# Attention and feed-forward layer on one core: queries in three buffers of two mirrored blocks, output projection as three rounded passes, three shared PSUM banks

## The reference, cut to what matters

```
xn = _layernorm(x, axis=-1)
q = einsum('bld,dhk->blhk', xn, Wq)            # 16 heads of 64
latent = einsum('bld,dc->blc', xn, Wkv_down)   # 64
k = einsum('blc,chk->blhk', latent, Wk_up)
v = einsum('blc,chk->blhk', latent, Wv_up)
attn = softmax(where(causal, einsum('bqhd,bkhd->bhqk', q, k) / sqrt(64), min))
y = einsum('bhqk,bkhd->bqhd', attn, v)
x = x + einsum('bqhd,hdo->bqo', y, Wout) + tanh(xn @ weight @ aux1 @ aux2 + bias)
```

## Time and profile before

| | |
|---|---|
| runs | 2118.16, 2114.27, 2122.21 us, median 2118.16 |
| the profiled execution | 2116.38 us, of which the recorded span is 2114.6 us |
| granted TensorE clock, mean | 0.997 |
| busy share of the span | PE 97%, DVE 71%, POOL 62%, ACT 49% |

### The profile page before, as it was taken

How to read it: one execution, slowest core, us unless ns; L and a number is a source line. 1 busy time by engine, 2 the same in 40 slices (tenths; PEclk the granted TensorE clock), 3 DMA queues, 4 the chain that set the end, 5 groups by cost and what they waited for, 6 DMA issues and landing times.

```text
span 2114.6 us, 32583 instructions
## 1 busy us (share of the span) xinstructions
PE 2042.4 (97%) x9912; PEld 1265.4 (60%) x9912; DVE 1501.8 (71%) x3743; ACT 1044.1 (49%) x1947; POOL 1319.9 (62%) x1163
## 2 busy tenths in 40 slices
PE   6999999999999999999999999999999999999997
PEld 5655666656666566656565656665666556666654
DVE  5868766787677776777676776778757687677662
ACT  4544554545545454544554545455554445545443
POOL 0666666666667565665666666667666566666765
PEclk9999999999999999999999999999999999999999
DMA  3111111211112111111111111111111111111111
GB/s 109 26 36 51 31 45 43 55 37 38 43 36 59 42 36 41 40 48 44 34 49 39 52 34 39 46 42 51 29 49 47 36 50 31 44 52 36 32 31 41
DMA packets 66999, 91.18 MB, mean 43 GB/s; under 512 B 12304, under 2 KB 33680, under 8 KB 66832
## 3 DMA queue, kind: packets, MB, share of 16 engines
q1 hardware_dynamic: 66832, 89.11, 15.3%
HBM read 45.55 MB, written 8.91 MB: 26 GB/s over the span
## 4 chain that ended last, share of the span: by engine, by line
PE 72%; DVE 16%; issue 4%; DMA 2%; ACT 2%; SPq 1%; POOL 0%; POOLq 0%; DVEq 0%
PE ps L860 20%; PE ps L874 12%; PE ps L843 10%; PE ps L911 10%; PE ps L846 9%; PE ps L814 8%; DVE maxima L1093 3%; PE ps L901 3%; DVE ps L1088 2%; DVE norm L1110 2%; DVE xn L1172 2%; DVE rows L1104 1%; DVE q_lo L1196 1%; DMA rows<-norm 1%; ACT q_hi L1064 1%
## 5 line engine op out<-in xcount | busy, mean ns | idle before, releaser
L1225 POOL TENSOR_TENSOR p_sum<-p_sum,probs 128x512 f32<-128x512 f32 x672 | 867.6, 1316 | 326.3 <-ACT probs L1010 325.5
L1010 ACT ACTIVATE probs<-ps 128x512 f32<-128x512 f32 x1152 | 673.2, 597 | 494.3 <-PE ps L846 467.1
L1088 DVE CUSTOM_DVE_ANT_0 ps<-ps,causal 128x256 f32<-128x256 f32 (+3 forms) x1024 | 495.5, 502 | 215.3 <-PE ps L874 206.5
L860 PE MATMUL ps<-probs,latent 128*64 128x512 f32 x2304 | 541.1, 601 | 0.0
L843 PE MATMUL ps<-q_hi,k_hilo 128*128 128x512 f32 x1152 | 499.4, 434 | 9.3 <-ACT probs L1010 9.1
L874 PE MATMUL ps<-k_hilo,q_hi 128*128 128x512 f32 (+3 forms) x1536 | 481.4, 368 | 19.1 <-DVE maxima L1088 11.0
L1093 DVE TENSOR_REDUCE maxima<-ps 128x1 f32<-128x512 f32 x512 | 351.4, 686 | 158.9 <-PE ps L874 156.7
L846 PE MATMUL ps<-q_lo,k_ones 65*128 65x512 f32 x1152 | 456.0, 396 | 0.0
L874 PEld LDWEIGHTS ps<-k_hilo,q_hi 128*128 128x128 f32 x1536 | 277.6, 189 | 176.2 <-issue 55.4
L1225 POOL TENSOR_TENSOR p_sum<-probs 128x512 f32<-128x512 f32 x224 | 292.2, 1321 | 131.5 <-ACT probs L1010 130.6
L1213 POOL TENSOR_SCALAR_AFFINE_SELECT probs<-probs 128x512 f32<-128x512 f32 x256 | 162.9, 639 | 316.3 <-ACT probs L1010 314.8
(11 more groups left out here) (93 smaller groups left out, 1488.5 us busy)
## 6 DMA issues: line engine op xcount, KB each, us to landing
q_hi<-q_hi SPq DMA_DIRECT2D x256, 128.0 KB, 2.3
norm<-recips SPq DMA_DIRECT2D x256, 128.0 KB, 2.9
x_in<-in_L_attn_x_bld SPq DMA_DIRECT2D x8, 1024.0 KB, 5.5
out_x<-acc SPq DMA_DIRECT2D x64, 128.0 KB, 1.7
q_lo<-rows SPq DMA_DIRECT2D x128, 4.0 KB
rows<-norm SPq DMA_DIRECT2D x128, 4.0 KB
recips<-rows SPq DMA_DIRECT2D x128, 4.0 KB
probs<-in_L_attn_Wq SPq DMA_DIRECT2D x1, 1024.0 KB, 8.0
```

The source lines that it names most:

```text
L860: last = nc.tensor.matmul(y_bank[g * LATENT:(g + 1) * LATENT, :], latent[par][:, key_block(unit, s), :], probs[:, t % PT_SLOTS, g * BANK:( ...
L1010: nc.scalar.activation(probs[:, t % PT_SLOTS, g * BANK:(g + 1) * BANK], st_bank[(2 * t + g) % ST_BANKS], ACT.Exp).then_inc(exp_done, 1)
L1088: nc.vector.tensor_tensor_reduce(bank, bank, causal[:, BANK - w:BANK], 1.0, LOWEST, ALU.add, ALU.max, maxima[:, unit % 4, h, 0:1]).then_in ...
L1225: nc.gpsimd.tensor_tensor(sums, other, probs[:, slot, part], ALU.add).then_inc(pool_done, 1)
```

## The change

1. **Order of units.** `HALF_BLOCKS` = (3,4), (2,5), (1,6), (0,7). Two units of mirrored blocks are a half (9 steps always), and a pair of blocks is done for the first octet, then for the second. Queries are made a half at a time (2 blocks, 8 heads) into one of three buffers, two halves ahead. A Q item now makes 4 heads of 2 blocks: 12 matmuls of 256 columns instead of 6 of 512. There are as many Q items (128), copies, remainders and DMAs as before, with the same elements.
2. **Output projection.** O is done in three rounded passes with `wvo_hi`, `wvo_lo`, `split_hi`, `split_lo`: 12 rounded matmuls of 256 columns for a unit instead of 4 in plain float32. For it NM writes back into `y`, then ACT rounds `y` to `split_hi` (HI), then DVE subtracts (LO) into `split_lo`; each once for a unit, 128x512. The prologue makes `wvo_lo` with four DVE subtractions.
3. **Banks.** Values (Y), preparation (P0) and small products (P1) share banks 5, 6 and 7; the planner gives each product the bank that is free first (`HOMES`, `takes`, `leaves`), and PE waits for the last reader of that bank alone (`bank_left`). A batch of PV steps may run across the end of a unit, since the next unit takes another bank.
4. **Planner.** `BATCH` 5, `LEAD` 13, other assumed times, an O after NM, HI and LO; the load of the next batch is put at step 30 of a batch instead of 32.

```diff
-SEGMENT_BLOCKS = [[3, 7, 4, 0], [5, 6, 2, 1]]
+HALF_BLOCKS = [(3, 4), (2, 5), (1, 6), (0, 7)]
...
-ST_BANKS, PT_SLOTS, Y_SLOTS, SUM_SLOTS = 2, 7, 3, 2
+PT_SLOTS, Y_SLOTS, SPLIT_SLOTS, SUM_SLOTS, Q_BUFS = 7, 3, 2, 2, 3
+HOMES = {"ST": (0, 1), "MAX": (2, 3, 4), "Y": (5, 6, 7), "P0": (5, 6, 7), "P1": (5, 6, 7)}
...
-BATCH = 4
+BATCH = 5
 SOON = 60
-LEAD = 12
+LEAD = 13
...
             elif kind == "NM":
+                self.multiplied[key] = self.run("DVE", when, DVE_TIME[kind])
+                if key < SPLIT_SLOTS or key - SPLIT_SLOTS in self.out:
+                    self.after(self.multiplied[key], "HI", key)
+            elif kind == "HI":
+                self.after(self.run("ACT", when, ACT_TIME[kind]), "LO", key)
+            elif kind == "LO":
                 self.normal[key] = self.run("DVE", when, DVE_TIME[kind])
                 self.outs.append((self.n_st / 2, key))
...
-            if s == block_of(u):
+            if s == block_of(u) and len(HOMES["Y"]) == 1:
                 return n, True
...
-            def p1_ready():
-                if n_p1:
-                    pe.wait_ge(p1_free, n_p1)
+            def bank_left(bank):
+
+                kind, key = last_use.get(bank, (None, None))
...
+                elif kind == "Y":
+                    pe.wait_ge(y_copied, key + 1)
+                elif kind in ("T", "K", "Q"):
+                    pe.wait_ge(p0_free, count.residual(kind, key) + 1)
...
                 elif kind in ("O0", "O"):
 
                     if kind == "O0":
-                        p1_ready()
-                        pe.wait_ge(y_normal, key + 1)
-                    for j in (0, 1) if kind == "O0" else (2, 3):
-                        last = nc.tensor.matmul(p1_bank[:, 0:D], norm[:, key % Y_SLOTS, j * P:(j + 1) * P],
-                                                wvo[:, octet_of(key) * PAIRS + j, :],
-                                                start=(j == 0), stop=(j == PAIRS - 1))
+                        p1_bank = take_bank("O", key)
+                        pe.wait_ge(norm_lo, key + 1)
+                    p1_bank = ps[:, bank_of["O", key], :]
+                    slot, first = key % SPLIT_SLOTS, octet_of(key) * PAIRS
+                    last = three_passes(
+                        p1_bank[:, 0:D],
+                        lambda a, j: (split_hi, split_lo)[a][:, slot, j * P:(j + 1) * P],
+                        lambda b, j: (wvo_hi, wvo_lo)[b][:, first + j, :],
+                        chunks=(0, 1) if kind == "O0" else (2, 3), of=PAIRS)
...
                     t, unit, s = key
                     act.wait_ge(pv_done, t + 1)
                     if unit >= Y_SLOTS:
-                        act.wait_ge(y_normal, unit - Y_SLOTS + 1)
+                        act.wait_ge(norm_lo, unit - Y_SLOTS + 1)
...
+                elif kind == "HI":
+                    act.wait_ge(y_normal, key + 1)
+                    if key >= SPLIT_SLOTS:
+                        act.wait_ge(p1_full, count.p1("O", key - SPLIT_SLOTS) + 1)
+                    nc.scalar.activation(split_hi[:, key % SPLIT_SLOTS, :], y[:, key % Y_SLOTS, :],
+                                         ACT.Copy).then_inc(norm_hi, 1)
...
+                elif kind == "LO":
+                    slot = key % SPLIT_SLOTS
+                    dve.wait_ge(norm_hi, key + 1)
+                    nc.vector.tensor_tensor(split_lo[:, slot, :], y[:, key % Y_SLOTS, :],
+                                            split_hi[:, slot, :].bitcast(F32),
+                                            ALU.subtract).then_inc(norm_lo, 1)
...
-        run(first_plan(), [ps[:, 6, :], ps[:, 0, :], ps[:, 1, :]], load_all, make_constants)
-        run(body_plan(B), [ps[:, 6, :]])
+        run(*first_plan(), load_all, make_constants)
+        run(*body_plan(B))
```

More of the change, by code:

```diff
@@ L274, in place_max @@
         self.plan.append(("MAX", self.maxima[self.n_max]))
+        self.takes("MAX", "MAX", self.maxima[self.n_max])
         slot = max(0.42 * w + 16, 112)
@@ L301, in place_p1_half @@
         self.plan.append(("O", u))
-        self.out.add(u)
-        self.p1_free = self.run("DVE", self.on_pe("O", ready), DVE_TIME["O"])
+        done = self.on_pe("O", ready)
+        self.out[u] = done
+        if u + SPLIT_SLOTS in self.multiplied:
+            self.after(max(done, self.multiplied[u + SPLIT_SLOTS]), "HI", u + SPLIT_SLOTS)
+        self.leaves("O", u, self.run("DVE", done, DVE_TIME["O"]))
     def place_f(self, ready):
@@ L308, in place_f @@
         self.n_f += 1
-        self.p1_free = self.run("DVE", self.on_pe("F", ready), DVE_TIME["F"])
-        self.after(self.p1_free, "FT", key)
+        self.takes("P1", "F", key)
+        end = self.run("DVE", self.on_pe("F", ready), DVE_TIME["F"])
+        self.leaves("F", key, end)
+        self.after(end, "FT", key)
     def place_r(self, ready):
@@ L315, in place_r @@
         self.plan.append(("R", u))
-        self.p1_free = self.run("ACT", self.on_pe("R", ready), ACT_TIME["R"])
-        self.after(self.p1_free, "RG", u)
+        self.takes("P1", "R", u)
+        end = self.run("ACT", self.on_pe("R", ready), ACT_TIME["R"])
+        self.leaves("R", u, end)
+        self.after(end, "RG", u)
     def place_p0(self, ready):
@@ L414, in build @@
             st = [c for c in usable if c[1] is None]
-            idle_act = self.free["ACT"] < now + 300
+            idle_act = self.free["ACT"] < now + 100
             late = max(due, key=lambda c: step - c[1], default=None)
@@ L439, in body_plan @@
 def body_plan(batches):
-    return Order(batches).build()
+    order = Order(batches)
+    plan = order.build()
+    return plan, order.bank
 def first_plan():
@@ L1273, in sync_program @@
                                  ).then_inc(x_loaded, 16)
-            for j in range(PAIRS):
-                sp.wait_ge(q_twice[j], 32 * sum(k == "Q" and key[1] == j for k, key in plan))
+            for i in range(Q_BUFS):
+                for j in range(2):
+                    uses = sum(k == "Q" and key[0] % Q_BUFS == i and key[1] == j for k, key in plan)
+                    if uses:
+                        sp.wait_ge(q_twice[i][j], 32 * uses)
             turned = sum(k == "MT" for k, _ in plan)
@@ L1280, in sync_program, with run @@
             if outputs:
-                for s in range(2):
-                    sp.wait_ge(stored[s], 16 * outputs // 2)
-        def run(plan, p0_banks, load=None, make_constants=None):
+                for s in range(BLOCKS // 2):
+                    sp.wait_ge(stored[s], 16 * outputs // (BLOCKS // 2))
+        def run(plan, bank_of, load=None, make_constants=None):
             with nc.Block() as block:
```

449 lines of the change are left out of this document (260 added, 189 removed).

## The result

The changed kernel takes 2100.57 us (median of 5, 2095.43 to 2103.03); the kernel before, in the same rounds, 2120.61 (median of 5). The ratio is 0.990, with a 95% interval from 0.988 to 0.992: 20 us less, where 54 were forecast. The direction was right and the time lies within the range for 8 in 10 (2040 to 2110), but outside the forecast's own (2046 to 2086): most of the forecast gain is missing. The profiled execution took 2102.5 us, with a span of 2100.8.

The account below looks back on a forecast made before the run. PE, busy for 97% of the span, was taken to set the pace. 2116.38 - 64 (PE work) + 20 (LO) - 15 (banks) + 5 (end) = 2062.4, median 2064 us; own range 2046 to 2086, 8 in 10 2040 to 2110.

Parts of the forecast that it names:

- What bounds the kernel: Whole body: PE, busy 97% of the span, sets the pace; cuts count fully unless what replaces them makes PE wait.
- Part 1: Output projection on PE: twelve rounded matmuls at 0.118 us replace eight recorded ones at 0.216; 40 us saved.
- the rival of the weight loads: O and Q on PE: weight loads of 189 ns in a row set the pace; 2281 us, chance 0.02.
- Their busy share: Weight loads on PE: 1280 more loads of 189 ns take their busy share from 60% to 73%.
- Parts 2 and 3: PE: twelve query matmuls instead of six, 3 us more; fewer changes of the array's form, 27 us saved.
- Part 4: HI on ACT hidden; LO adds 130 us on DVE, PE's waits for maxima grow by a half: +20 us.
- the second rival: NM, HI, LO queues: the planned order slips, 0.38 us lost on PE a unit; 2108 us, chance 0.10.
- LO as PE's limit: DVE's queue: LO ahead of maxima costs PE its 1.02 us each; 2190 us, chance 0.11.
- Part 5: Shared banks: PE's waits of Q and O for a bank, 28 us, go by half; -15 us.
- Part 6: Kernel's end: POOL's last steps +1.4 us, HI and LO behind NM +1.2, PE's 2.4 saved hidden; +5 us.
- for longer than 1.03: Sign for the end: R of the last unit waits longer for POOL than 1.03 us.

Follow-up runs that it names:

- e2: Changed kernel with the output projection as before (8 float32 matmuls, no HI, no LO), order built anew; 2093.9 us, ratio to before 0.987.
- e9: Changed kernel, same order, LO replaced in place by two bn_stats of one SBUF input, lower halves left out of O; 2061.4 us, ratio to before 0.972.
- e1: Changed kernel, same order, without DVE's LO; O reads the upper halves in both roles; 2051.2 us, ratio to before 0.967.
- e8: Kernel before with the layer-norm chain of batches 1 to 7 left out; 2116.5 us, ratio to before 0.9995.
- e3: Changed kernel, same order, layer-norm chain after bn_aggr left out in batches 1 to 7; 2069.1 us, ratio to before 0.976.
- e11: Changed kernel with float32 output projection as before and the layer norm's Newton steps on POOL; 2073.8 us, ratio to before 0.978.
- e4: Changed kernel with one bank each for values, preparation and small products; 2122.9 us, ratio to before 1.002.
- e12: Changed kernel, same order, without both LO and the layer-norm chain of batches 1 to 7; 2030.6 us, ratio to before 0.959.
- e14: e11 with Newton links spread behind POOL's additions and the first batch's chain on DVE; 2078.6 us, ratio to before 0.982.
- e7: Changed kernel with LO on POOL instead of DVE, order built anew; 2085.2 us, ratio to before 0.985.

## Why the prediction was wrong in size, step by step

- **What bounds the kernel** held: PE paces the body. What was not held is the other half of that sentence, "unless what replaces it makes PE wait".
- **Part 1**, 40 us less work: 39 (e2 against after, by counts and pitches). The rounded matmuls follow each other at 0.12 us in the trace after; the rival of the weight loads is refuted. Their busy share rose to 63%, not 73%: the records of loads overlap, so 1280 more of them can't be added up whole.
- **Parts 2 and 3**, together 24 us less work: 24 (63 less 39). Both by the rows read ahead; the 4.44 us of five PV steps came out exactly.
- **Part 4 is the step that failed**: +20 forecast for LO, 47 to 48 measured. The term was sized by LO's mean time on DVE and by DVE's share of busy time. e9 shows that this part costs 10 us. The other 38 are that LO and POOL's additions stop each other. The prediction named the rule and NM's spread as evidence, and then priced LO at the mean of NM, as if the spread were already all of it. Yet LO came to 1.12 us in the mean instead of 1.02, and it lengthened POOL's 672 sums by 0.03 us each (e1); NM it left alone. Per unit, PE lost 47 / 128 = 0.37 us. That is the figure of the second rival, the order that slips (0.38), and its 2108 us came nearest, but by luck: the chain of three queues that it blames costs at most e9's 10 us or so. LO as PE's limit (from 0.46 us a unit on) did not come.
- **A term is missing**: the layer-norm chain, nothing in the kernel before (e8), 28 to 31 us after (e3). The prediction took all instructions that the change doesn't touch at their old durations, and gave no reason. The new order set twelve short ones beside POOL's additions.
- **Part 5**, -15 for bank waits: without LO and with the Newton steps off DVE, waits are 87 us (e11) against 116 in before, 29 less. So more was to be had than forecast, and the chain took it back: e2, with the chain, has before's 115. That it is the sharing of banks is not shown: with a bank for each there was no more waiting but 5 us less (e4), in an order that had moved in other ways too. The mirrored blocks, `LEAD`, the third buffer and two thresholds of the planner (300 ns, now 0 and 100) change at the same time and were not taken apart.
- **Part 6**, +5 at the end: POOL is busy for 27.60 us in a stretch of 30 shortly before the end instead of 26.51, and O waits for 10.0 us for the last LO. But R waited for POOL for 0.58 us, not for longer than 1.03, and from the last R to the end it took 2100.8 - 2083.7 = 17.1 us instead of 2114.6 - 2095.1 = 19.5. So the traces show the greater load and not the cost; its size was not tried on its own.
- With the terms at their measured sizes: 63 us less work, +47 for LO, +28 for the chain, -29 for the other waits: -17 us, where the body of the profiled execution gave 41 - 63 = -22 (and the medians -20). The terms may overlap (e12), and -29 is itself read from a run without most of the other two, so this shows that they suffice, not that each is exact.

## What to carry to other kernels

Price a new DVE instruction with two SBUF inputs beside a POOL that adds by what it stops and what stops it, not by its own length; a chain of short dependent ones was the worst case here, since each link can wait for a whole addition. When an order is built anew, look at what untouched instructions come to stand next to. Before giving up a part that "brings nothing", take its side cost away: the rounded output projection was worth nothing with LO on DVE, and 31 to 40 us with LO on POOL and the links spread.

## What the runs showed of the hardware

- A DVE `TENSOR_SCALAR` with one SBUF input of 128x8, also on int32, waited for POOL's addition as those with two inputs did: 0.17 us alone, some 1.2 beside additions in a row, once 1.78 (after, L1258). One of 128x256 took 0.40 to 1.36 us (e14, L1284). `bn_stats` of 128x256, also one SBUF input, did not wait: 0.401 to 0.430 us as LO's stand-in (e9), and POOL's sums were at 1.336, as without LO.
- Where DVE kept PE idle for 2 to 7 us, the granted clock mostly fell to the lower level (1.2 GHz) for 3.4 to 10.2 us around the stall: in e7 seven such stretches of 6.8 to 10.2 us, one a batch, in e12, without the stalls, none between 61 us and the end. One stall of 2.2 us in after (at 957 us) brought none. Behind e7's stall at 694 us, matmuls of 512 columns start 0.43 us apart (696.17 and 696.60) instead of 0.23. So such a stall can cost more than its length.
- The prologue varies on its own: the same instructions brought the first ST at 53.8 or at 60.7 us, with 3.4 or 20.5 us at the lower clock. Of one profiled execution this is no reading of a change.
